# Local attention in two layers: scores from contractions of 64 rows, maxima and exponentials of eight heads at once, and a new order of the attention period

## The reference, cut to what matters

```python
def local_attention(q, k, v):                 # 8 heads of 64, window 64
    bq = q.reshape(b, h, w, WINDOW, d) * QK_SCALE
    bk, bv = (look_around(bk), look_around(bv))     # the block and the one before it
    sim = jnp.einsum('bhwid,bhwjd->bhwij', bq, bk)
    mask = (i < j) | (i > j + WINDOW) | (j == -1)
    sim = jnp.where(mask, -jnp.finfo(sim.dtype).max, sim)
    attn = jax.nn.softmax(sim, axis=-1)
    out = jnp.einsum('bhwij,bhwjd->bhwid', attn, bv)

def _layer(x, ...):                           # run twice
    h = shift_token(x)
    q, k, v = jnp.split(h @ wqkv, 3, axis=-1)
    q = l2norm(q) * qs; k = l2norm(k) * ksc
    q, k = rotary_xpos(q, k)
    x = x + local_attention(q, k, v) @ wo
    ...                                       # shift, norm, gated feed-forward
```

## Time and profile before

| | |
|---|---|
| median of 3 runs | 2178.75 us (2176.16 to 2181.96) |
| the profiled execution | 2176.2 us |
| its span, first to last instruction | 2174.4 us |
| mean granted clock of PE | 0.929 of 2.4 GHz |
| busy share of the span | PE 82%, DVE 75%, ACT 58%, POOL 44% |

### The profile page before, as it was taken

The page is one execution under the profiler, slowest core; times in us unless marked ns, Lnnn a source line. Parts: engine busy times, 40 slices in busy tenths (PEclk is TensorE's granted clock), DMA queues, the critical chain, the costliest instruction groups (busy, mean ns, idle before and its releaser), DMA issues. The chain is left out here.

```text
span 2174.4 us, 36880 instructions
## 1 busy us (share of the span) xinstructions
PE 1781.2 (82%) x12448; PEld 976.1 (45%) x12448; DVE 1635.1 (75%) x3467; ACT 1271.2 (58%) x2737; POOL 957.9 (44%) x773
## 2 busy tenths in 40 slices
PE   5888898865889998859943757999998899999875
PEld 2333333332344444424423424655655556566543
DVE  5999999995577777622235767999986689999775
ACT  5777877740344444414434236888884388888721
POOL 5777887761012222223431245555550255555311
PEclk8999999996899999959976878999999999999997
DMA  5333333312111111114235140000001000000010
GB/s 150 110 111 119 122 108 116 93 49 81 39 37 36 41 36 44 31 41 133 65 105 165 52 137 15 16 21 16 11 16 23 13 16 21 16 16 11 15 42 23
DMA packets 107401, 125.47 MB, mean 58 GB/s; under 512 B 28804, under 2 KB 79151, under 8 KB 106224
## 3 DMA queue, kind: packets, MB, share of 16 engines
q1 hardware_dynamic: 103120, 115.07, 18.7%
q0 software_dynamic: 4096, 8.06, 1.1%
HBM read 71.60 MB, written 38.11 MB: 50 GB/s over the span
## 5 line engine op out<-in xcount | busy, mean ns | idle before, releaser
L394 POOL TENSOR_TENSOR m_bu<-m_dtu,m_brow 128x1024 f32<-128x1024 f32 x128 | 299.8, 2358 | 55.6 <-DVE m_hs L818 53.9
L818 DVE TENSOR_TENSOR_SCAN m_hs<-m_ps_da,m_bu 128x1024 f32<-128x1024 f32 x128 | 292.3, 2283 | 3.0 <-POOL m_bu L394 2.5
L1363 ACT ACTIVATE a_pt<-a_ps_s 128x1024 f32<-128x1024 f32 x128 | 131.1, 1024 | 226.7 <-PE a_ps_s L1141 226.7
L523 PE MATMUL m_ps_y_ps<-m_prod,m_ident 128*128 128x512 f32 x512 | 243.1, 597 | 0.0
L2913 ACT ACTIVATE l_pe<-l_ps_s,l_nbias,l_qs 128x128 f32<-128x128 f32 x512 | 227.9, 459 | 1.6
L1480 DVE TENSOR_REDUCE a_mpad<-a_ps_s 128x4 f32<-128x1024 f32 x128 | 156.9, 1226 | 92.3 <-PE a_ps_s L1133 91.1
L1133 PE MATMUL a_ps_s<-a_heads 32*128 32x256 f32 x1024 | 187.5, 446 | 43.6 <-DVE a_mpad L1480 28.5
L670 ACT ACTIVATE m_ps_da<-m_dt,m_a_neg 128x510 f32<-128x510 f32 x256 | 166.0, 681 | 74.3 <-DVE m_hs L818 73.4
L1141 PE MATMUL a_ps_s<-a_qm,a_heads 32*128 32x256 f32 x1024 | 184.7, 437 | 1.8 <-ACT a_pt L1363 1.4
L1067 POOL TENSOR_TENSOR a_rstd<-a_ve,a_mhalf 128x2 f32<-128x2 f32 x48 | 33.8, 705 | 303.0 <-DVE a_ve L1438 163.3
L828 DVE TENSOR_TENSOR m_prod<-m_hs,m_ps_c_ps 128x1024 f32<-128x1024 f32 x128 | 153.6, 1200 | 12.1 <-PE m_ps_c_ps L509 12.1
(11 more groups left out here) (339 smaller groups left out, 4252.1 us busy)
## 6 DMA issues: line engine op xcount, KB each, us to landing
m_brow<-state_rows SPq DMA_DIRECT2D x64, 512.0 KB, 4.3
slots<-m_void SPq DMA_DIRECT2D x16, 516.0 KB, 5.4
l_near<-l_v SPq DMA_DIRECT2D x64, 128.0 KB, 2.3
e_xs<-slots SPq DMA_DIRECT2D x16, 258.0 KB, 2.8
ys<-m_void SPq DMA_DIRECT2D x8, 512.0 KB, 5.3
qk<-a_qk SPq DMA_DIRECT2D x16, 256.0 KB, 2.0
a_heads<-qk SPq DMA_DIRECT2D x64, 64.0 KB
ew_w<-in_w SPq DMA_DIRECT2D x2, 2048.0 KB, 11.8
```

The source lines that it names most:

```text
L394: nc.gpsimd.tensor_tensor(bu[s % 4][:, :, :], dtu[p][:, :, :], b2, ALU.mult).then_inc(bu_rd, 1)
L523: last = pe.matmul(y_ps[:, h, :], ident[:, :], prod[d % 3][:, h, :], start=False, stop=(s == NS - 1))
L818: dve.tensor_tensor_scan(hs[s % 4][:, :, :].rearrange("p h t -> p (h t)"), da[s % 2][:, :, :, :].rearrange("p h q t -> p (h q t)"), bu[s % ...
L1363: nc.scalar.activation(pt[t % 2][:, :, :], s2[:, :, :], ACT.Exp).then_inc(exp_rd, 1)
```

## The change

It edits `phase_local` only.

- Scores: `kT` has its plain size, with no zeros. A contraction has 64 rows, one head: the head of a pair with rows 0 to 63 writes into bank 0 of `s_ps`, the one with rows 64 to 127 into bank 1. `scores` now does all eight heads of a chunk, and the mask goes in twice for each chunk.
- `maxima` takes eight heads over two banks in one reduction, and the eight exponentials of a chunk stand in one stretch.
- From the third chunk of queries and the second of keys on, `turn_q` and `turn_k` write into `t_ps[1]` and `t_ps[0]`, the banks of the transposed probabilities, and no longer into `qk_ps`. `c1` gets two buffers for each of queries and keys.
- `k_copy` is one copy of 128 rows where there were two of 64.
- Each engine's `attend` is written anew as a loop over the two chunks.

```diff
-        s_ps = [m.ps(f"s{i}") for i in range(2)]
+        s_ps = m.ps("s", (P, 2, 512))
+        kept = {Q: 2, K: 1}
+        def turned(i, x):
+            return qk_ps[:, x, :] if i < kept[x] else t_ps[1 - x][:, :]
...
+                def scores(n, b, c):
+                    pe.wait_ge(l.xT_sb[Q], i + 1)
+                    pe.wait_ge(l.xT_sb[K], i + 1)
+                    at_least(pe, l.ex_rd, NH * i)
+                    for r in range(2):
+                        pe.matmul(bank[r], identb[:, :], mask[:, c, :, :], start=True, stop=False, skip_group_check=True)
+                    for j in range(NP):
                         if c == 0:
+                            for r in range(2):
+                                last = pe.matmul(bank[r][:, j, :], qT[p][side[r], j, 0:P], kT[p][side[r], j, 0:P],
+                                                 start=False, stop=True, skip_group_check=True)
                         else:
+                            for q in range(2):
+                                q0 = P + q * HD
+                                for r in range(2):
+                                    last = pe.matmul(bank[r][side[q], j, :], qT[p][side[r], j, q0:q0 + HD],
+                                                     kT[p][side[r], j, q0 - HD:q0 + HD], start=False, stop=True,
+                                                     skip_group_check=True)
...
                 def attend(n, b, first=False, last=0):      # PE
+                    for c in range(NCH):
+                        scores(n, b, c)
+                        before = (b, 0) if c == 1 else (b - 1, 1)
+                        behind = not first or c == 1
+                        if c == 1 and last < 1:
+                            pe.wait_ge(l.v_sb, NCH * (b + 1) + 1)
+                            transpose_r(n, b + 2)
+                        if behind:
+                            transpose_p(n, before[0], NU * before[1])
+                        if last < 2:
+                            project(n, b + 1, c, Q)
+                            project(n, b + 1, c, K)
+                        if behind:
+                            transpose_p(n, before[0], NU * before[1] + 1)
+                        if not first:
+                            ...
+                            output(n, b - 1, c)
+                        if behind:
+                            weigh(n, before[0], NU * before[1])
+                        if c == 0:
+                            turn_k(n, b, 1)
+                        elif last < 2:
+                            turn_k(n, b + 1, 0)
+                        if last < 2:
+                            if not first:
+                                pe.wait_ge(l.res_rd, NCH * (b - 1) + c + 1)
+                            else:
+                                pe.wait_ge(l.hT_sb, 2 * (b + 2 + c))
+                            project_v(n, b + 1, c)
+                        if behind:
+                            weigh(n, before[0], NU * before[1] + 1)
+                        if last < 2:
+                            turn_q(n, b + 1, c)
...
                 def attend(n, b, first=False, last=0):      # ACT
+                    for c in range(NCH):
+                        ...                                 # before, behind as above; shift in chunk 1
+                        if behind:
+                            p_copy(n, before[0], NU * before[1])
+                        exps(n, b, NU * c)
+                        exps(n, b, NU * c + 1)
+                        if behind:
+                            p_copy(n, before[0], NU * before[1] + 1)
+                        if c == 0:
+                            k_copy(n, b, 1)
+                        elif last < 2:
+                            k_copy(n, b + 1, 0)
+                        if last < 2:
+                            square(n, b + 1, c, Q)
+                            square(n, b + 1, c, K)
+                            v_copy(n, b + 1, c)
+                        if behind:
+                            o_copy(n, *before)
+                        if last < 2:
+                            q_copy(n, b + 1, c)
...
                 def attend(n, b, first=False, last=0):      # DVE
+                    for c in range(NCH):
+                        summed = (b, 1) if c == 0 and not first else (b + 1, 0) if c == 1 and last < 2 else None
+                        if summed:
+                            square_sums(n, *summed, K)
+                        maxima(n, b, c)
+                        if summed:
+                            square_sums(n, *summed, Q)
+                        if last < 2:
+                            rotary(n, b + 1, c, Q)
+                        if c == 0:
+                            scale_k(n, b, 1)
+                        elif last < 2:
+                            scale_k(n, b + 1, 0)
+                        else:
+                            norm_stats(n, 0)
+                        if last < 2:
+                            rotary(n, b + 1, c, K)
+                            rotary_sum(n, b + 1, c, K)
+                        divide(n, b, NU * c)
+                        if not first:
+                            residual(n, b - 1, c)
+                        divide(n, b, NU * c + 1)
```

More of the change, by code:

```diff
@@ L2716, in attend @@
                     l = at[n]
[L2717 to L2738, removed]
-                        if last < 2:
-                            pe.wait_ge(l.v_sb, NCH * (b + 1) + 1)
-                        else:
-                            pe.wait_ge(l.res_rd, NCH * (b - 1))
-                        output(n, b - 1, 0)
-                        weigh(n, b - 1, U - 1)
@@ L2760, in attend @@
-                    if last < 2:
-                        turn_k(n, b + 1, 0)
-                    scores(n, b, 3)
-                    if last < 2:
-                        project(n, b + 1, 1, K)
-                    transpose_p(n, b, 1)
-                    if last < 2:
-                        turn_q(n, b + 1, 1)
-                    if not first:
-                        if last == 0:
-                            pe.wait_ge(l.hT_sb, 2 * (b + 3))
-                        elif last == 1:
-                            pe.wait_ge(l.v_sb, NCH * (b + 2))
-                        else:
-                            pe.wait_ge(l.res_rd, NCH * (b - 1) + 1)
-                        output(n, b - 1, 1)
@@ L3092, in attend @@
                 def attend(n, b, first=False, last=0):
-                    if not first:
-                        divide(n, b - 1, U - 2)
-                        square_sums(n, b, 1, K)
-                    maxima(n, b, 0)
-                    if last < 2:
-                        rotary(n, b + 1, 0, Q)
-                    scale_k(n, b, 1)
-                    if not first:
-                        divide(n, b - 1, U - 1)
-                    maxima(n, b, 1)
-                    if last < 2:
-                        square_sums(n, b + 1, 0, Q)
-                        rotary(n, b + 1, 0, K)
-                        rotary_sum(n, b + 1, 0, K)
@@ L3108, in attend @@
-                    if not first:
-                        residual(n, b - 1, 0)
-                    divide(n, b, 0)
-                    if last < 2:
-                        square_sums(n, b + 1, 0, K)
-                    maxima(n, b, 2)
-                    if last < 2:
-                        rotary(n, b + 1, 1, Q)
-                        scale_k(n, b + 1, 0)
-                    else:
-                        norm_stats(n, 0)
-                    divide(n, b, 1)
-                    maxima(n, b, 3)
```

176 lines of the change are left out of this document (66 added, 110 removed).

## The result

The changed kernel takes 2241.36 us (2240.19 to 2244.52), the kernel before, run beside it, 2177.45 (2175.56 to 2181.96). The ratio is 1.029, 95% interval 1.028 to 1.031: slower, as forecast, but by 64 us where 19 were forecast, and above the upper end of the range, 2232.

What follows compares the result with a forecast made beforehand. Local attention was taken as bound by a circle of waits between DVE and PE, 10.56 us a chunk. +22 (circle) +7 (array parts) -18 (ends) +8 (clock) = +19 us gave 2198 us, range 2160 to 2232.

Steps and rivals of the forecast that it cites:

- The circle: Local attention: DVE's and PE's halves wait for each other without overlap, 10.56 us a chunk, 0.40 more than before, +22 us.
- VectorE's half: DVE's stretch of each chunk, from the start of the maxima to the end of the residual: 6.90 us.
- PE's half: PE's stretch from the residual over `project_v`, `weigh`, `turn_q`, masks and scores to the next maxima: 3.66 us.
- The array's parts: Chunk 1's scores: 32 passes on four array parts, at least three at once, 1.1 us; +0.25 in 28 chunks, +7 us.
- Rival 5: Scores: 64-row products don't run side by side, or only in pairs in chunk 1; 2207 to 2250 us, chance 0.07.
- the rule: The skill's drain at a tiling mode change, around the scores; by it the sum would be about 8 us higher.
- The clock: PE's pauses of 2.4 us in 10.6 lower its granted clock; +8 us taken, between bounds of nothing and +41.
- Rival 4: PE's clock falls after most pauses, as in the feed-forward window: +41 us, 2231 us in all, chance 0.12.
- The ends: Periods 0 and 15 of each layer get shorter, by 4 and 5 us; twice 9 is -18 us.
- The divisions: On DVE they move away from POOL's addition, all near 0.69 us, so the loss of 0.86 us a chunk goes.

Runs made afterwards that it cites:

- e1: The changed kernel with the residual moved on VectorE from behind the first division to right behind `scale_k`; ratio to the kernel before 0.967.
- e5: The changed kernel with the residual early and contractions of 128 rows, keys beside zeros, in place of 64-row parts; ratio to the kernel before 1.007.
- e3: The changed kernel with an unused projection product added in PE's pause before `project_v` in each chunk; ratio to the kernel before 1.0145.
- e8: The changed kernel with the residual early and `turn_q` not waiting for the queries' square from the third chunk on; ratio to the kernel before 0.955.
- e9: The changed kernel with residual early, second unit's probabilities copied between the exponential groups, and `turn_q` not waiting for the square; ratio to the kernel before 0.952.

## Why the prediction was right in its sign and wrong in its size

**The circle: right.** `project_v` waits for the residual, the maxima for the scores behind `project_v`, and nothing in the wait counts opens the circle. VectorE's half was forecast at 6.90 us and is 6.90. Experiment e1 shows that it is the cause, since moving its last link alone gives back more than the whole loss.

**PE's half: 3.66 forecast for chunk 0, 3.93 measured.** `project_v` is 1.05 and not 0.97, `turn_q` 0.49 and not 0.43, scores with way and wake 1.21 and not 1.07. Rows of a projection and of transposes that follow their like came out 0.06 to 0.08 too short for their places here. In chunk 1 the sum forecast, 3.66 and 0.25 for its parts, was 3.91, and 3.92 was measured, but by luck: the same rows are too short there, and the 0.25 didn't come. Over 56 chunks: +37 where +22 and +7 were forecast, so 8 us.

**The array's parts: sized too high.** All four parts of 64 rows by 64 columns run at once: 32 passes take 1.10 us with the way through, 16 passes in pairs 1.16. I took three. With 0.25 less for chunk 1 the term of +7 is none, and what filled its place was the term above. Rival 5, that such products run one by one or in pairs, is out.

The Trainium skill, "TensorEngine Tiling (Array Packing)", Key Properties, has the array drain at a change of tiling mode. This case agrees in part: the first divided product starts 0.31 us after the second mask, where the full products of e5's chunk 0 start 0.22 after theirs. So the change costs about 0.1 us, which was in the sum, and less than the 0.17 of the way through. The change back stands behind the last score and so outside the circle. The +8 us of the rule are not there.

**The clock: the step that failed most.** "I take +8, since transposes and scores follow close on each other here", between bounds of nothing and +41. It is +28. I had the row that speaks of it, pauses of 2.25 us in 11 and a clock of 0.93, called the pauses alike, and then took a fifth of its price. That transposes and scores follow close after the pause didn't help: the clock fell 1.0 to 1.6 us after work was taken up, in the midst of PE's half, and that half is on the circle with all its 1.56 us. Experiment e3 prices it by itself, at 1.3 to 1.5% of the time. With +28 in place of +8 the forecast would have been 2218, inside the range. Rival 4, at 2231, would have been 10 us off in place of 43, but in part by luck: it let the clock fall after most pauses, for 41 us, and it fell after 18 of 56; and it gave back 18 us at the ends that didn't come.

**The ends: -18 forecast, -5 measured, the second step that failed.** I counted 4 for each period 0 and 5 for each period 15. Period 0 gave 1.3 and 2.0. VectorE doesn't set it alone: its two chunks take 8.32 and 9.00 us where I had 7.4 and 8.0. Without the wait for the square they take 8.1 to 8.3 and 8.4 (e8), or 8.15 and 8.25 (e9), so of the 1.9 us too much 0.6 to 0.9 are the row of ScalarE's work that I had not followed because the circle hid it elsewhere. What sets the rest stays open. In period 15 the way from the first mask to the last four transposes of probabilities is 16.4 us in the first layer and 18.2 in the second, where the clock falls in the scores, against 20.27 before and 15 forecast. But ahead of its last eight transposes PE waits 3.18 us for a copy of probabilities that stands behind eight exponentials, then its clock falls, and the transposes that open the feed-forward part start 4.0 us after those eight began, where it was 1.2 after the last four before. So 1.6 us are left in the first layer and nothing in the second. The timeline of TensorE:

```profile
1673.59 0.66 PE L2713 MATMUL l_ps_o<-l_pT,l_v 128*64 128x128 f32 x8 [3.18 <-ACT l_pT L2920]
1674.17 1.31 PE L2693 MATMUL l_ps_t<-t_ident,l_pn 128*128 128x128 f32 x8
1675.28 1.91 PE L2730 MATMUL l_ps_a<-t_wo,l_oT 128*128 128x128 f32 x8
...
1678.18 0.70 PE L2782 MATMUL l_ps_qk<-t_ident,l_hn 128*128 128x128 f32 x4
```

**The divisions: right.** All take 0.69 us, where 58 of 128 took 1.55 before, as the one in the earlier trace rows. No run prices this by itself. In the changed kernel VectorE waits more than that in each chunk anyway.

The misses add up: 8 for the circle, 20 for the clock, 13 for the ends and 3.5 outside the stage, 45 us, as between the 19 forecast and the 64 measured. The time forecast, 2198, was 43 too low, since the kernel before took 1.3 us less beside the changed one.

## What to carry to other kernels

Follow one shared buffer round all engines before counting what each engine saves: VectorE had a tenth less to do here and the kernel got 3% slower, because the read of a bank stood at the end of its row, and the next write of that bank ahead of the work on PE for which VectorE waits next. Look where in its engine's order the releasing instruction stands, and put it as early as its input allows. And where the work behind a new pause of PE is on the path, price the pause by the nearest one whose clock is in the trace, and not by a small part of it: here 41 us by that row, 8 taken, 28 measured. A pause shortened or filled can cost less than one left open.

## What the runs showed of the hardware that I had not expected

- A pause of 2.0 to 2.2 us in 10.8 was followed by 1.2 GHz in one chunk of three; two of about 0.8 and 0.2 us, or of about 0.8 and 0.6, in none. A product of 1.1 us that serves nothing, put into each pause, saved 28 us.
- Filling every second pause saved nothing: 19 falls, all behind the pauses left open.
- Four parts of 64 by 64 work fully side by side: 32 passes of 128 columns in 1.10 us, where 16 passes in two parts take 1.16 and eight of 256 columns over all rows 1.89.
